# Halves' sums of y kept in free columns of two score banks instead of SBUF, with score bursts that wait for them

## The reference

```python
x = x + tanh(g_xattn) * (attention(layernorm(x), ctx) @ Wo.T + bo)    # 16 heads of 32, causal softmax
x = x + tanh(g_ffn) * (top-6 of 8 experts + a shared expert)(layernorm(x))
```

## Time and profile before

| what | value |
|---|---|
| time, median of 3 runs | 1872.62 us (1871.63 to 1873.6) |
| the profiled execution's own time | 1871.45 us |
| its span, first to last instruction | 1869.7 us |
| PE busy | 1785.5 us (95%) |
| DVE busy | 1420.5 us (76%) |
| ACT busy | 963.3 us (52%) |
| POOL busy | 926.1 us (50%) |

### The profile page before, as it was taken

One profiled execution on the slowest core, in us unless ns is written; L12 is line 12 of the kernel. 1 busy time (PEld: TensorE's weight loads), 2 busy tenths in 40 slices (PEclk: granted clock), 3 DMA queues, 4 the chain that ended last, 5 costly groups with the idle time before them and its releaser, 6 DMA issues.

```text
span 1869.7 us, 33758 instructions
## 1 busy us (share of the span) xinstructions
PE 1785.5 (95%) x11904; PEld 1488.6 (80%) x11904; DVE 1420.5 (76%) x3101; ACT 963.3 (52%) x2260; POOL 926.1 (50%) x1185
## 2 busy tenths in 40 slices
PE   6899999999996899999999999999999999999999
PEld 6788878878885678888778888877888887888887
DVE  6777877887777677777977777788777788777776
ACT  5888888888887424333533343443333444333331
POOL 4776777777667433433533344444343453333330
PEclk9999999999996999999999999999999999999999
DMA  4778888877886412121141221123212112211111
GB/s 149 139 148 171 145 169 163 167 158 152 175 165 141 145 57 69 56 71 54 34 158 46 79 68 57 46 78 115 79 46 79 45 57 99 93 46 56 46 46 45
DMA packets 301000, 182.84 MB, mean 98 GB/s; under 512 B 210080, under 2 KB 265376, under 8 KB 300832
## 3 DMA queue, kind: packets, MB, share of 16 engines
q1 hardware_dynamic: 300832, 180.69, 38.7%
HBM read 111.43 MB, written 18.87 MB: 70 GB/s over the span
## 4 chain that ended last, share of the span: by engine, by line
PE 69%; DVE 15%; issue 6%; ACT 4%; POOL 3%; DMA 2%; SPq 1%; DVEq 0%; POOLq 0%; ACTq 0%
PE gate_up L1292 32%; PE down L1807 19%; PE bank L789 13%; DVE ops_lo L1149 2%; DVE acc L1658 2%; ACT probs L597 2%; POOL hidden L1506 1%; PE scores L895 1%; DVE y L677 1%; DVE x_in L641 1%; PE y_values L917 1%; DVE stats L621 1%; PE rows_t L779 1%; PE y_values L915 1%; DVE y_sum L673 1%
## 5 line engine op out<-in xcount | busy, mean ns | idle before, releaser
L1292 PE MATMUL gate_up<-xo_hi,ops_hi 128*128 128x512 f32 x1120 | 440.6, 393 | 13.0 <-DVE hidden L1268 4.5
L1292 PE MATMUL gate_up<-xo_hi,ops_lo 128*128 128x512 f32 x1120 | 436.7, 390 | 0.0
L1292 PE MATMUL gate_up<-xo_lo,ops_hi 128*128 128x512 f32 x1120 | 436.5, 390 | 0.0
L487 POOL TENSOR_TENSOR halves<-probs,halves 128x384 f16<-128x384 f32 x244 | 226.7, 941 | 85.5 <-ACT halves L591 84.4
L1658 DVE SCALAR_TENSOR_TENSOR acc<-down,scale,acc 128x512 f32<-128x512 f32 x320 | 238.5, 746 | 34.8 <-PE down L1807 34.3
L1292 PEld LDWEIGHTS gate_up<-xo_hi,ops_hi 128*128 128x128 f32 x1120 | 210.5, 188 | 66.5 <-DVE gated L1268 9.6
L597 ACT ACTIVATE probs<-probs,neg_max 128x128 f32<-128x128 f32 (+1 forms) x512 | 229.0, 449 | 56.8 <-DVE neg_max L719 56.8
L1506 POOL TENSOR_TENSOR hidden<-hidden,gated 128x512 f32<-128x512 f32 x120 | 157.4, 1319 | 189.8 <-DVE hidden L1273 170.4
L1807 PE MATMUL down<-d_hi,h_hi 128*128 128x512 f32 x640 | 249.1, 389 | 0.0
L1807 PE MATMUL down<-d_hi,h_lo 128*128 128x512 f32 x640 | 249.0, 389 | 0.0
L1807 PE MATMUL down<-d_lo,h_hi 128*128 128x512 f32 x640 | 249.0, 389 | 0.0
(11 more groups left out here) (182 smaller groups left out, 4240.3 us busy)
## 6 DMA issues: line engine op xcount, KB each, us to landing
g_raw<-in_w_gate SPq DMA_DIRECT2D x40, 512.0 KB, 3.5
u_raw<-in_w_up SPq DMA_DIRECT2D x40, 512.0 KB, 3.5
d_raw<-in_w_down SPq DMA_DIRECT2D x40, 512.0 KB, 3.4
c_in<-in_ctx_t SPq DMA_DIRECT2D x16, 512.0 KB, 4.5
x_in<-in_x SPq DMA_DIRECT2D x16, 512.0 KB, 6.0
x_res<-in_x SPq DMA_DIRECT2D x16, 512.0 KB, 4.9
x_between<-x_res SPq DMA_DIRECT2D x16, 512.0 KB, 3.4
acc<-x_between SPq DMA_DIRECT2D x32, 256.0 KB, 4.0
```

What stands on the lines that cost most here:

```text
L487: pool.tensor_tensor(halves[k % HALVES][:, 1, :], probs[k % RING][:], halves[k % HALVES][:, 0, :], ALU.subtract).then_inc(p_lo_made, 1)
L1292: ins = pe.matmul(gu_ps[bank][:], ops[x][:, which, a, c, :], xo[y][:, b, c, :], start=(begins and c == 0 and i == 0), stop=(c == CH - 1 an ...
```

## The change

The sums of the two halves go to columns 0 to 127 of the first two score banks, one bank for each of the two query tiles `t`. The four banks become one tensor, so that one instruction can write both. The sums of the last two groups of the last batch stay in SBUF (`is_tail`). A score burst also waits until the group whose sums lie in the banks has been closed: the burst of group G waits for the `y` of group G - 3.

```diff
-    sc_ps = [psum(f"scores{j}", [P, P + 3 * P]) for j in range(JH)]
+    scores = psum("scores", [P, JH, P + 3 * P])
+    sc_ps = [scores[:, j, :] for j in range(JH)]
     y_ps = psum("y_values", [P, T, JH, 2, DH])
     rows_ps = psum("rows_t", [P, D])
+    y_sum_ps = scores[:, 0:T, 0:P].rearrange("p t (h d) -> p t h d", d=DH)
...
+    def is_tail(b, g):
+
+        return b.k == B - 1 and g >= H // JH - 2
...
                 dve.reciprocal(row_inv[:], row_sum[:, heads, :]).then_inc(group_chain, 1)
-                dve.tensor_reduce(y_sum[:], y_ps[:].rearrange("p t h x d -> p (t h) d x"), AX.X,
+                whole = y_sum[:].rearrange("p (t h) d -> p t h d", t=T) if is_tail(b, g) else y_sum_ps
+                dve.tensor_reduce(whole, y_ps[:].rearrange("p t h x d -> p t h d x"), AX.X,
                                   ALU.add).then_inc(group_chain, 1)
...
                 dve.tensor_tensor(y[:, part, :, at:at + P].rearrange("p t (h d) -> p t h d", d=DH),
-                                  y_sum[:].rearrange("p (t h) d -> p t h d", t=T),
+                                  whole,
                                   row_inv[:].rearrange("p h t -> p t h").unsqueeze(3).to_broadcast([P, T, JH, DH]),
                                   ALU.mult).then_inc(y_made, 1)
...
                 wait(pe, max_made, head(i, JH * g))
+                wait(pe, y_made, i.times(H // JH, g - H // JH + 2))
```

## The result

| what | before | after |
|---|---|---|
| time, median | 1873.11 us (1871.63 to 1873.64, 4 runs) | 1857.38 us (1855.64 to 1861.52, 4 runs) |
| the profiled execution's own time | 1871.45 us | 1857.01 us |
| its span | 1869.7 us | 1854.7 us |

The changed kernel is faster by 0.8%: the ratio is 0.992, with a 95% interval from 0.9904 to 0.9935. That is 15.7 us by the medians, where 4.85 were forecast.

The account below looks back on a forecast made before the run. PE was taken as the bound, waiting for DVE 1.97 us per iteration. Gains of 0.28 + 0.17 over 13 iterations, 5.85 us, less 1.0 in the last batch, gave 4.85 us faster: 1867.8 us, range 1862 to 1872.5.

Parts of the forecast that it names:

- `y` at 0.424 everywhere: DVE's multiplication in the closings: with one input in PSUM it takes 0.424 us everywhere, where it took up to 1.524.
- The reduce: DVE's reduce of 512 elements to 256 sums: writing them to PSUM changes its 0.640 us by 0.
- The rival of a long reduce: Writing into two score banks lengthens each closing; with 1.0 us more the time is 1879; chance 0.08.
- Slot 6, 0.28 per iteration: Closing ahead of the statistics: `y` ends 1.10 us earlier, but POOL holds the small steps, so `rstd` gains 0.28 us.
- Slot 10, 0.17 per iteration: Closing ahead of `x_in` and `t_lo`: one POOL lower half is no longer delayed, so both `x_in` end 0.17 us earlier.
- The added wait: Bursts waiting for their closing cost nothing in the middle and 1.0 us in the last batch, bounds 0 and 6.6.
- More is gained: Rival: POOL doesn't hold the small steps, all of 1.10 + 0.17 us comes off PE in 12 iterations: 1858.4; chance 0.08.
- no change: Rival: late loads or another link leave only slot 10's 0.17, the last batch costs 1 to 3: 1871.4 to 1873.4; chance 0.28.
- Slower: Rival: the write into two score banks lengthens each closing and bursts wait; 1879 us at 1.0 us more; chance 0.08.
- what was to be seen: Signs: short `y`, second `x_res` add at 1.29, no 1.10 lower half, PE's two waits from 23.3 to about 18 us.
- the signs by which the prediction would be wrong: `rstd` over 0.6 us earlier, bursts waiting mid-stage, reduce above 0.70 us, or last batch growing by more than 2 us.

Follow-up runs that it names:

- ACT's early release in the changed kernel: The changed kernel with ACT making the upper half that releases POOL's fourth lower half ahead of `t_hi`: 1865.53 us, ratio 0.9958.
- ACT's delay in the kernel before: The kernel before with an extra 128-column ACT copy ahead of the upper half that releases POOL's fourth lower half: 1868.76 us, ratio 0.9973.
- ACT's two instructions exchanged: The kernel before with ACT making the upper half that releases POOL's fourth lower half ahead of `t_hi`: 1873.03 us, ratio 0.9998.
- wait-only kernel: The changed kernel with all sums kept in SBUF, so that only the bursts' wait for the closing remains: 1876.09 us, ratio 1.0015 to the kernel before.

## Why the prediction was wrong in size

**`y` at 0.424 everywhere: right.** 48 closings of the middle lie between 423 and 426 ns. Of the VectorE: DVE Perf Modes page of the Trainium skill, section on the TRN2 errata, by which a source in PSUM costs 62 cycles more than one in SBUF (120 against 58), nothing shows here: 424 ns with the sums in PSUM, 424 at least without.

**The reduce: nearly.** Nothing was taken for the write into PSUM; it costs 7 ns. The rival of a long reduce falls.

**Slot 6, 0.28 per iteration: the mechanism right, the size a little high.** The chain of holds ran as worked out, with `var_eps` behind the second `x_res` add and the next step behind POOL's lower half. In the iteration shown `rstd` ends 3.58 us behind the start of `y`, in the earlier trace rows 3.99: 0.41 earlier, where 0.39 was worked out. Where the load is in time, PE's wait falls from 0.75 to 0.37, in four others to 0.54 to 0.57; over all 12 iterations the gain is 0.21, because DVE waits for the load in nine of them and not in one.

**Slot 10, 0.17 per iteration: this step failed.** It read "POOL's row of four sets their end, and `t_lo` follows". The 0.17 itself came: where the halves stand in one row again (ACT's early release in the changed kernel) the two `x_in` take 2.03 us instead of 2.20, and `t_lo`'s wait is 1.0 instead of 1.2. What the sum had at nothing is the order within the row. The row has a seam: its fourth half isn't set by the third but by ACT, 0.12 to 0.16 us behind it in the kernel before; the earlier trace rows counts the four as one piece, because the idle time is that short. And the two engines don't stand in a fixed order at that seam: the one that comes first goes first. Taking 0.17 off the third half let the second `x_in` come ahead of the fourth half instead of behind it, so that it no longer waits for a whole lower half. This change of order is worth 0.60 us: from 2.20 to 1.60 where it alone is brought about (ACT's delay in the kernel before), from 2.03 to 1.42 between the early release and the changed kernel. With both, the term measured 0.83. Delaying the fourth half gives the new order to the kernel before, releasing it early takes it from the changed one, and neither touches `y`: that shows the order to be the cause. `t_lo`'s wait gave 9.1 us where 13 by 0.17 are 2.2: 6.9 of the 10.9 us missed.

**The added wait: right in the middle, wrong in the last batch.** No burst waits in the middle. In the last batch 1.0 us was taken for a loss, and 0.8 were gained. That recurs: from the first burst of batch 15 to `gate_up` the kernel before takes 39.82 us in its profiled execution and as much with ACT's two instructions exchanged; the changed kernel takes 39.06, and the six kernels built on it in the later experiments 37.95 to 39.06. Two windows that cover the same stretch, from the first burst of batch 15 to `gate_up`, before and after (busy us of each engine, then the granted clock):

```profile
563.90:603.70 39.80, 23.45 (x308) 19.28 (x308) 30.02 (x95) 31.57 (x97) 31.46 (x25) 0.61 0.68 139
```

```profile
550.90:590.00 39.10, 21.60 (x307) 18.19 (x308) 30.01 (x91) 31.70 (x97) 31.10 (x25) 0.65 0.67 141
```

PE is busy for 1.85 less on as many matmuls, at a granted clock of 0.65 instead of 0.61. Its idle time grew from 16.35 to 17.50 us. That this is near the forecast 1.0 is luck, as is shown below. The clock's part stands near the end, in five of these us in which PE is busy throughout:

```profile
593.77:598.75 4.98, 4.98 (x45) 3.87 (x45) 2.38 (x12) 4.81 (x17) 2.15 (x4) 0.51 0.92 112
```

```profile
580.26:585.15 4.89, 4.89 (x51) 3.95 (x50) 3.38 (x16) 4.72 (x16) 1.79 (x3) 0.88 0.48 92
```

Before, PE came out of idling 2.86 and 1.31 us and worked at the 1.2 GHz level nearly all through this stretch; after, its last burst comes late and the matmuls behind it follow without such a gap, and most of the stretch is at 2.4 GHz. That the higher clock brings the work behind it forward is read from these windows and not tested. Only a part of it arrives. The `x_res` step of DVE that PE releases near the end (at 599.60 before, 584.45 after) starts 33.5 us behind the first burst of the batch instead of 35.7. Then DVE's lower halves meet POOL's `xo_lo`, before and after:

```profile
598.72 2.40 POOL L1094 TENSOR_TENSOR xo_lo<-t_sum,xo_hi 128x1024 fp32r<-128x1024 f32 x1
600.26 1.27 DVE L751 TENSOR_TENSOR halves<-probs,halves 128x384 f16<-128x384 f32 x1
```

```profile
585.01 2.39 POOL L1102 TENSOR_TENSOR xo_lo<-t_sum,xo_hi 128x1024 fp32r<-128x1024 f32 x1
585.11 2.71 DVE L758 TENSOR_TENSOR halves<-probs,halves 128x384 f16<-128x384 f32 x1
```

They come 0.10 behind its start now and stand through all of it, 2.71 us instead of 1.27; a closing follows them, and PE idles 1.87 us for its `y` instead of 0.43. So 1.4 of the 2.2 are lost again to POOL, and this growth of one wait is more than that of the whole idle time. The wait-only kernel, too, took 39.55 us from that burst to `gate_up`, 0.27 less than before, so in that execution the waits by themselves cost nothing there. Why its median is nevertheless 3 us above the kernel before isn't settled; in its profiled execution, the fastest of its ten, the thirteen batches of the middle took 2.2 us longer.

**The rivals.** "More is gained" came closest in time (1858.4) and was wrong in its reason: the small steps are held by POOL, as the 0.84 of `shifted` shows. Of "no change" one condition came about, loads late in most iterations (nine of twelve); it fell because slot 6 still gave 0.21 and slot 10 gave 0.83 where the rival had kept 0.17. "Slower" fell with the reduce. Of what was to be seen, PE's two waits came to 11.7 us and not about 18, and one long lower half remained, the fourth. None of the signs by which the prediction would be wrong came; none of them looked at slot 10.

**The rest of the 10.9 us.** Beside slot 10's 6.9 the last batch makes 1.8, the first two batches 1.5, the experts 1.3 and the difference between medians and profiled executions 0.7; slot 6 gave 1.1 less than its 13 by 0.28, and the middle is 0.2 less than its two waits. Over the profiled executions of this study the first two batches and the experts vary by more than they give here.

## What to carry to other kernels

Where two engines share something, look not only at how long each holds the other but at who comes first at each meeting, and by how much: here 0.1 us decided over 0.6, thirteen times, and an edit that saved 0.17 paid nearly five times that. A group of instructions that a view counts as one row may have a seam inside; ask for each of its members what released it. A delay on an engine that isn't critical made one kernel here 5.3 us faster, and earlier work made the other some 7 us slower (by the ratios to the kernel before), so it is worth trying both on chip before a larger edit.

## What the runs showed that I had not expected

- A DVE step on two elements was held for nearly as long as POOL's whole instruction ran: `var_eps` took up to 889 ns and `shifted` up to 847, against 168 undisturbed. Each of the twelve that took over 400 in the middle of the changed kernel ended 23 to 28 ns behind a POOL instruction.
- An `x_in` of 512 columns that was held ended 0.28 to 0.29 us behind POOL's instruction. In its turn it stretched a lower half from 0.92 to 1.19 us, and a POOL step on two elements to 0.37 to 0.40, where Newton's steps of that size take 0.19 to 0.20.
